# Block-quantised feed-forward: maxima one iteration ahead, scales on GpSimd, gated values three iterations behind

## What is computed

```python
def fp4_quant_dequant(x):                  # blocks of 16 columns
    xb = x.reshape(shape[:-1] + (shape[-1] // 16, 16))
    scale = jnp.maximum(jnp.max(jnp.abs(xb), axis=-1, keepdims=True) / 6.0, 1e-12)
    xn = xb / scale
    idx = jnp.searchsorted(_MID, jnp.abs(xn))
    return (_GRID[idx] * jnp.sign(xn) * scale).reshape(shape)   # grid 0 0.5 1 1.5 2 3 4 6

def fp4_linear(x, w):
    return jnp.einsum('bsk,nk->bsn', fp4_quant_dequant(x), fp4_quant_dequant(w))

h = jax.nn.silu(fp4_linear(x, w_gate)) * fp4_linear(x, w_up)    # 128 -> 352
return fp4_linear(h, w_down)                                    # 352 -> 128
# x = x + 0.5 * ffn(layernorm(x))
```

## Time and profile before

| | us |
|---|---|
| median of 3 runs (1597.82 to 1600.06) | 1597.97 |
| span of the profiled execution | 1594.8 |
| what the median has beside the span | 3.2 |
| first feed-forward, first block maxima to last statistics | 138.24 |
| second feed-forward, the same | 138.29 |
| busy over the span: TensorE, VectorE, ScalarE, GpSimd | 1233.0, 996.9, 714.1, 593.8 |

### The profile page before, as it was taken

How to read it: one execution, slowest core, us unless ns; L and a number is a source line. 1 busy time by engine, 2 the same in 40 slices (tenths; PEclk the granted TensorE clock), 3 DMA queues, 4 the chain that set the end, 5 groups by cost and what they waited for, 6 DMA issues and landing times.

```text
span 1594.8 us, 31915 instructions
## 1 busy us (share of the span) xinstructions
PE 1233.0 (77%) x10217; PEld 799.1 (50%) x10218; DVE 996.9 (63%) x1974; ACT 714.1 (45%) x1328; POOL 593.8 (37%) x859
## 2 busy tenths in 40 slices
PE   0677479999956776299999915999998728999992
PEld 0355346666634556156666602455554525666661
DVE  5799679999838994822222257889896382223233
ACT  0444225555554442144444451666666323444445
POOL 2122221121101220056565614676775104656561
PEclk9989769999988996589999956999999658999996
DMA  8000034223200001011111133434242101111115
GB/s 254 9 0 0 1 61 63 49 53 60 43 2 1 0 0 53 2 36 42 40 39 40 41 112 67 68 56 79 56 75 34 54 0 32 40 40 41 38 41 171
DMA packets 161956, 75.54 MB, mean 47 GB/s; under 512 B 126539, under 2 KB 153940, under 8 KB 161876
## 3 DMA queue, kind: packets, MB, share of 16 engines
q1 hardware_dynamic: 152404, 55.06, 16.1%
q0 software_dynamic: 9472, 19.42, 4.1%
HBM read 28.69 MB, written 15.86 MB: 28 GB/s over the span
## 4 chain that ended last, share of the span: by engine, by line
PE 54%; DVE 25%; issue 7%; ACT 6%; POOL 3%; DMA 3%; SPq 1%; DVEq 1%; POOLq 0%; ACTq 0%
PE PS L990 16%; PE PS L1016 9%; PE PS L656 4%; PE PS L1006 4%; PE PS L358 2%; DVE sg L790 2%; DVE m L790 2%; PE PS L622 2%; PE PS L638 2%; PE PS L575 2%; PE PS L951 2%; DVE q_amax L266 2%; PE PS L610 1%; ACT pt L1070 1%; SPq L882 1%
## 5 line engine op out<-in xcount | busy, mean ns | idle before, releaser
L990 PE MATMUL PS<-wgu,xTs 128*128 x584 | 303.2, 603 | 4.2 <-issue 3.1
L1114 DVE TENSOR_TENSOR pt<-pt,PS 128x512 f32<-128x512 f32 x146 | 100.5, 688 | 295.4 <-PE PS L990 295.4
L715 ACT ACTIVATE pt<-PS 128x768 f32<-128x768 f32 (+1 forms) x256 | 227.5, 917 | 107.8 <-PE PS L638 56.1
L1227 POOL DMA_INDIRECT xs<-rows,src x152 | 147.8, 972 | 192.9 <-DVE src L1108 147.1
L1236 POOL DMA_INDIRECT outs<-ys,dst x144 | 142.4, 989 | 158.5 <-DVE ys L1122 153.0
L1052 ACT ACTIVATE pt<-PS 128x512 f32<-128x512 f32 x146 | 87.2, 597 | 233.8 <-PE PS L990 233.8
L1016 PEld LDWEIGHTS PS<-wdn,pt 128*128 128x128 f32 x1152 | 139.5, 191 | 55.4 <-issue 55.4
L1016 PE MATMUL PS<-wdn,pt 128*128 x1152 | 162.9, 284 | 0.4 <-issue 0.4
L790 DVE TENSOR_REDUCE m<-PS 128x4 f32<-128x1024 f32 x128 | 149.1, 1218 | 10.5 <-PE PS L575 9.9
L575 PE MATMUL PS<-tables 64*128 64x128 bf16 (+2 forms) x1536 | 131.7, 251 | 0.0
L790 DVE TENSOR_REDUCE sg<-PS 128x6 f32<-128x768 f32 x128 | 117.6, 953 | 20.9 <-PE PS L575 20.0
(11 more groups left out here) (229 smaller groups left out, 2239.5 us busy)
## 6 DMA issues: line engine op xcount, KB each, us to landing
pt<-outs SPq DMA_DIRECT2D x16, 512.0 KB, 5.0
rows<-qT SPq DMA_DIRECT2D x12, 256.0 KB, 2.4
xs<-rows,src POOLq DMA_INDIRECT x152, 2.5
outs<-ys,dst POOLq DMA_INDIRECT x144, 2.3
wgu<-in_L_ffn_w_gate SPq DMA_DIRECT2D x1, 2048.0 KB
wgu<-in_L_ffn_w_up SPq DMA_DIRECT2D x1, 2048.0 KB
wdn<-in_L_ffn_w_down SPq DMA_DIRECT2D x8, 256.0 KB
qT<-hqT SPq DMA_DIRECT2D x128, 4.0 KB
```

Of the source, the lines that this page charges most:

```text
L715: s.activation(k.pt[:, a % 4, :, 0:w], k.PS[:, self.bank:self.bank + 2, 0:w], ACT.Exp, scale=self.scale).then_inc(self.s_p, 1)
L990: t.matmul(k.PS[:, 1 + 2 * p + w, :], k.xTs[:, p, :], k.wgu[:, w, ds(e, 1), :].squeeze(1), start=True, stop=True).then_inc((self.s_gate_ps ...
L1114: v.tensor_tensor(k.hs[:, p, :], k.sgs[:, p, :], k.PS[:, 2 + 2 * p, :], ALU.mult).then_inc(self.s_h, 1)
L1227: g.indirect_dma_start(k.xs[:, i % RING, :], None, k.rows[:, :], bass.IndirectOffsetOnAxis(ap=k.src[:, i:i + 1], axis=0)).then_inc(self.s_ ...
```

## The change

Four things are rearranged inside `Ffn`; the arithmetic stays, apart from the order in which the inverse and its factors are multiplied.

1. The block maxima of iteration z + 1 are taken during iteration z, between the gate and the roundings, and their reciprocal directly after them (of the maximum, no more of the scale).
2. The scales, and the inverses' constant factor, are computed by GpSimd (`scales`), ahead of its dequantisations of iteration z. VectorE's multiplication waits for them (`s_inv`).
3. The gated values are rounded three iterations behind x instead of two. On VectorE the order is now multiplication, gate, maxima of the next iteration, roundings, addition.
4. On TensorE the order is now transposes of x, transposes of the gated values, the first half of gate and up, down, the second half. ScalarE's order follows: copy of x, squares, copies of the gated values, normalisation of z + 3, silu.

The diff, without the constructor's new semaphores and the changed loop bounds (N + 4 steps instead of N + 5, four passes of the loop instead of five):

```diff
     def vector(self, eng, ch):
...
-            ch.run(v.tensor_reduce(amax, blocks, AX.X, ALU.max, apply_absolute_value=True))
...
-            ch.run(v.tensor_scalar(scale, amax, -1.0 / 6.0, -1e-12, ALU.mult, ALU.min))
-            ch.run(v.reciprocal(inv, scale))
-            ch.run(v.tensor_scalar(inv, inv, -NUDGE, None, ALU.mult))
-            last = v.tensor_tensor(xn.rearrange("p (n k) -> p n k", k=BLK), blocks,
-                                   inv.unsqueeze(2).broadcast_to([P, n, BLK]), ALU.mult)
-            last.then_inc(self.s_xn_read, 1)
+        def largest(z, p):
+            c = self.cols(z)
+            if self.has(z):
+                eng.wait_ge(self.s_xn, x0 + z + 1)
+            if self.has(z - 3):
+                eng.wait_ge(self.s_h, x0 + z - 2)
             b = slice(c.start // BLK, c.stop // BLK)
...
+            ch.run(v.tensor_reduce(k.qt["amax"][:, b], blocks(k.fxh[p][:, c]), AX.X, ALU.max, apply_absolute_value=True))
+            v.reciprocal(k.qt["inv"][:, b], k.qt["amax"][:, b]).then_inc(self.s_amax, 1)
+        largest(0, 0)
 
         def fn(z, p):
-            if self.has(z) or self.has(z - 2):
-                quantised(z, p)
+            if self.group(z):
...
+                eng.wait_ge(self.s_inv, q0 + z + 1)
+                v.tensor_tensor(blocks(xn), blocks(k.fxh[p][:, c]),
+                                k.qt["inv"][:, b].unsqueeze(2).broadcast_to([P, b.stop - b.start, BLK]),
+                                ALU.mult).then_inc(self.s_xn_read, 1)
+            if self.has(z - 2):
+                eng.wait_ge(self.s_silu, x0 + z - 1)
+                v.tensor_tensor(k.fxh[1 - p][:, HID:k.FW].rearrange("p (a b) -> p a b", a=2), k.sg[:, :, :],
+                                k.PS[:, 2:4, 0:I0], ALU.mult).then_inc(self.s_h, 1)
+            if self.group(z + 1):
+                largest(z + 1, 1 - p)
+            if self.group(z):
+                eng.wait_ge(self.s_sq, q0 + z + 1)
+                ch.run(v.scalar_tensor_tensor(xn, mg, BASE, xn, ALU.add, ALU.add))
+                v.scalar_tensor_tensor(mg, mg, BASE, xn, ALU.add, ALU.subtract).then_inc(self.s_rounded, 1)
             if self.has(z - 4):
                 self.add(eng, z - 4)
...
@@ gpsimd
+        def scales(z, p):
+            c = self.cols(z)
+            b = slice(c.start // BLK, c.stop // BLK)
+            scale = k.fscale[:, p, b]
+            eng.wait_ge(self.s_amax, q0 + z + 1)
+            if self.has(z - 2):
+                eng.wait_ge(self.s_xq, x0 + z - 1)
+            if self.has(z - 5):
+                eng.wait_ge(self.s_hq, x0 + z - 4)
+            eng.sem_inc(self.s_seen, 1)
+            inv = k.qt["inv"][:, b]
+            g.tensor_scalar(scale, k.qt["amax"][:, b], -1.0 / 6.0, -1e-12, ALU.mult, ALU.min)
+            g.tensor_scalar(inv, inv, 6.0 * NUDGE, 1e12 * NUDGE, ALU.mult, ALU.min).then_inc(self.s_inv, 1)
+        scales(0, 0)
...
-            x, h = self.has(z), self.has(z - 2)
+            x, h = self.has(z), self.has(z - 3)
+            if self.group(z + 1):
+                scales(z + 1, 1 - p)
             if x or h:
                 eng.wait_ge(self.s_rounded, q0 + z + 1)
...
@@ tensor, its new order
+            if x:
+                eng.wait_ge(self.s_xqT, x0 + z + 1)
+                if self.later(z):
+                    eng.wait_ge(self.s_h, x0 + z)
+                gate_up(0)
+            if h:
                 eng.wait_ge(self.s_hqT, x0 + z - 2)
                 if self.later(z - 3):
                     eng.wait_ge(self.s_added, x0 + z - 3)
...
                 last.then_inc(self.s_y_ps, 1)
             if x:
...
+                gate_up(1).then_inc(self.s_gu_ps, 1)
```

More of the change, by code:

```diff
@@ L202 @@
     N = NT // 2
[L203 removed]
+    STEPS, FIRST = N + 4, 4
     HID = 2 * D
@@ L233, in later, with group, cols @@
         return self.run or not isinstance(i, int) or i >= n
+    def group(self, z):
+        return self.has(z) or self.has(z - 3)
+    def cols(self, z):
+        return slice(0 if self.has(z) else self.HID, self.k.FW if self.has(z - 3) else self.HID)
     def walk(self, eng, fn, ch=None, per=0):
@@ L332, in tensor, with gate_up @@
         x0, HID = self.x0, self.HID
-        def fn(z, p):
-            x, h, down = self.has(z), self.has(z - 2), self.has(z - 3)
-            if down:
+        def gate_up(j):
+            for w, bank in ((0, 0), (1, 2)):
+                last = t.matmul(k.PS[:, bank + j, 0:I0], k.xqT[:, j * P:(j + 1) * P], k.wguT[:, w, :],
+                                start=True, stop=True)
+            return last
+        def fn(z, p):
+            x, h = self.has(z), self.has(z - 3)
+            if x:
+                eng.wait_ge(self.s_xq, x0 + z + 1)
+                if self.later(z):
+                    eng.wait_ge(self.s_xqT, x0 + z)
+                for j in range(2):
+                    last = t.transpose(k.PS[:, 4, j * P:(j + 1) * P], k.xhq[:, j * D:(j + 1) * D], k.ident[:, :])
+                last.then_inc(self.s_xqT_ps, 1)
+            if h:
+                eng.wait_ge(self.s_hq, x0 + z - 2)
+                if self.later(z - 3):
+                    eng.wait_ge(self.s_hqT, x0 + z - 3)
+                for j in range(2):
+                    for c, (o, w) in enumerate(HC):
+                        o += HID + j * I0
+                        last = t.transpose(k.PS[0:w, 5 + j, c * P:(c + 1) * P], k.xhq[:, o:o + w], k.ident[:, :])
+                last.then_inc(self.s_hqT_ps, 1)
+            if x:
+                eng.wait_ge(self.s_xqT, x0 + z + 1)
+                if self.later(z):
+                    eng.wait_ge(self.s_h, x0 + z)
+                gate_up(0)
+            if h:
                 eng.wait_ge(self.s_hqT, x0 + z - 2)
@@ L381, in normalised, with squared @@
             ins.then_inc(self.s_xn, 1)
+        def squared(z, p):
+            if self.group(z):
+                c = self.cols(z)
+                eng.wait_ge(self.s_xn_read, q0 + z + 1)
+                if self.has(z) and self.later(z, 2):
+                    eng.wait_ge(self.s_xq, x0 + z - 1)
+                if self.has(z - 5):
+                    eng.wait_ge(self.s_hq, x0 + z - 4)
+                s.activation(k.fmg[p][:, c], k.fxn[p][:, c], ACT.Square, scale=BINADE ** 0.5).then_inc(self.s_sq, 1)
         eng.wait_ge(self.k.sem("statistics_ready"), self.phase + 1)
@@ L385, in scalar @@
         normalised(1, 1)
-        def squared(z, p):
-            if self.has(z) or self.has(z - 2):
-                c = slice(0 if self.has(z) else HID, k.FW if self.has(z - 2) else HID)
-                eng.wait_ge(self.s_xn_read, q0 + z + 1)
-                if self.has(z) and self.later(z, 2):
-                    eng.wait_ge(self.s_xq, x0 + z - 1)
-                if self.has(z - 4) or (self.has(z - 2) and self.run):
-                    eng.wait_ge(self.s_hq, x0 + z - 3)
-                s.activation(k.fmg[p][:, c], k.fxn[p][:, c], ACT.Square, scale=BINADE ** 0.5).then_inc(self.s_sq, 1)
         squared(0, 0)
+        normalised(2, 0)
         def fn(z, p):
```

84 lines of the change are left out of this document (21 added, 63 removed).

## The result

| | us |
|---|---|
| kernel before, median of 13 runs (1597.55 to 1602.03) | 1598.97 |
| changed kernel, median of 13 runs (1600.02 to 1608.62) | 1604.61 |
| ratio, 95% interval | 1.0032 (1.0021 to 1.0042) |
| changed kernel, profiled span | 1602.1 |

The time lies in the predicted range, 1587 to 1606, but the forecast, 1596 and no change that can be told, is wrong: the kernel is slower by 3.4 to 6.7 us.

The account below looks back on a forecast made before the run. VectorE, 92% busy, bounds the stages: full steps 7.92 us against 7.82, but shorter steps at the ends save 0.9 us a stage. Span 1594.8 - 1.8 = 1593.0, plus 3.2, gives 1596 us; range 1587 to 1606.

Parts of the forecast that it names:

- the bound, and what is removed: Feed-forward stages: VectorE bounds the iteration; scales, factor, gap and wait for squares go, 0.90 us less, 6.92 undisturbed.
- the port: Way to SBUF that VectorE instructions with two SBUF operands and GpSimd instructions take in turns; the second asking waits.
- the collision: VectorE's multiplication waits for GpSimd's 704-column dequantisation and ends at 3.11 instead of 2.11 us, so steps take 7.92.
- the 704 columns: GpSimd's second dequantisation, of the gated values that down multiplies; forecast to go ahead of the multiplication.
- ends at R + 0.72, so the 704-column one is asked for about 0.25 us ahead: GpSimd's 256-column dequantisation, taken as 0.57 us, ends early enough for the 704-column one to precede VectorE's multiplication.
- R: End of VectorE's second rounding, from which the times of a step are counted.
- The small instruction: GpSimd's added instruction on 60 columns, for scales or factor: 0.3 us each, the second ending about R + 0.15.
- Rival one: Multiplication gets in front of the 704-column dequantisation or does not contend: steps of 6.92 to 7.1 us; chance 0.16.
- a late addition only uses up the time for which the multiplication would have waited anyway. I put this at nothing here: TensorE's slow-clock spells, adding up to about 2.4 us, cost nothing because the multiplication would wait at the port anyway.
- hidden room of down: TensorE's down ends at 6.87 us after the rounding, 0.97 us before the addition wants it at 7.84.
- start and end: Stage's filling and draining: first gate about 0.3 us later, shorter steps at both ends, last rounding to end unchanged, 6.40.
- rival two: Small GpSimd instructions land on VectorE's path: 0.1 to 0.5 us a full step, 1599 to 1608 us; chance 0.17.

Follow-up runs that it names:

- factor on ScalarE: Changed kernel with the inverses' factor moved from GpSimd to ScalarE, without the guard for a block of zeros: 1597.63 us, 0.9993 of the kernel before.
- busy TensorE: Changed kernel with TensorE also transposing the identity into unread PSUM columns in three of its waits: 1592.83 us, 0.9957 of the kernel before.
- addition behind the gate: Changed kernel with the addition and its statistics moved from behind the roundings to behind the next step's gate: 1620.47 us, 1.0141 of the kernel before.
- addition ahead of the roundings: Changed kernel with the addition, of the product five iterations back, between reciprocal and roundings on VectorE: 1595.80 us, 0.9983 of the kernel before.
- both orders changed: Kernel with VectorE's addition ahead of the roundings, with TensorE's and ScalarE's orders changed besides: 1580.89 us, 0.9881 of the kernel before.

## Why the prediction was wrong, point by point

**Right: the bound, and what is removed.** VectorE's own work and its waits at the port set the steps in which no addition waits for down. Where the multiplication isn't held off such a step is 6.89 us; the prediction took 6.92.

**Right: the collision.** Where the multiplication stands behind the 704 columns it takes 1.9 to 2.2 us and ends 1 us after them. With the factor on ScalarE all steps are of that kind, 7.87 us against the forecast 7.92, and the time is 1597.6 against 1596: the port's arithmetic was sound where its conditions held.

**The step that failed first: "ends at R + 0.72, so the 704-column one is asked for about 0.25 us ahead".** Three terms were a little short. The small instruction, priced 0.3, is 0.41 by itself (the undisturbed ones at 102.27 and 102.75 above), and 0.41 less the 0.14 of hidden start-up is the 0.28 that it ends behind R. A hand-over of 0.07 follows, counted as nothing. The 256 columns are 0.62, not 0.57. Together 0.13 + 0.07 + 0.05 = 0.25 us: the whole margin. Rival one was told with a single cause, a small instruction of 0.55 us; three small shortfalls do the same. Which of the two steps comes is then decided by the 0.2 us by which the loop's turn delays the multiplication.

**The step that failed second, and made it slower: "a late addition only uses up the time for which the multiplication would have waited anyway. I put this at nothing here".** Both the hidden room of down (0.97 us) and this cover belong to the step where the multiplication waits. Where it doesn't, the addition wants down 1.26 us sooner (R + 6.81, not R + 8.07), while the 704 columns end 1.0 us later and keep down about where it was: at the full clock it ends at R + 7.03 where the multiplication waits (step from R = 107.14), and at R + 6.88 where it doesn't (step from R = 100.25, the addition waits 0.15 us). In a slow spell the lower clock has its full price, 1.3 to 2.9 us. So in a slow spell the short step of 6.89 us is followed by a long one: 8.95 and 8.77 us in the first stage, 9.05, 10.18 and 9.88 in the second, where the clock is lowest; at the full clock by one of 8.15. A short and a long step together are 15.0 us where the addition waits 0.15 us, 15.8 where it waits 1.8, which is twice the forecast's 7.92, and 16.8 to 17.1 where it waits 2.9: of these pairs only the last lose against the forecast. The factor on ScalarE shows the other side: there the cover held, and waits of 0.59 to 0.74 us cost nothing. Rival one had the gain and a ring through silu, but not that the displaced 704 columns take down with them.

**Mis-sized: start and end.** Ten full steps of a stage are 78.3 and 83.2 us, forecast 79.2. The first of them alone is 10.03 and 10.34, because its addition waits 3.04 and 3.34 us. From the last rounding to a stage's end are 8.2 and 8.0 us, forecast as unchanged, 6.40. The last two downs both run at the lower level there (granted clock 0.50 from 168 to 178), where before the last one took 1.60 us. The changed kernel:

```profile
168.33 2.93 PE L393 MATMUL PS<-wdT,hqT 128*128 128x128 f32 x12 [0.95 <-ACT hqT L439]
...
171.30 0.42 DVE L306 SCALAR_TENSOR_TENSOR X<-PS,X 128x256 f32<-128x256 f32 x1 [2.10 <-PE PS L393]
...
173.50 2.93 PE L393 MATMUL PS<-wdT,hqT 128*128 128x128 f32 x12 [0.95 <-ACT hqT L439]
176.46 0.42 DVE L306 SCALAR_TENSOR_TENSOR X<-PS,X 128x256 f32<-128x256 f32 x1 [4.21 <-PE PS L393]
```

The kernel before:

```profile
175.26 1.60 PE L342 MATMUL PS<-wdT,hqT 128*128 128x128 f32 x12 [0.95 <-ACT hqT L418]
```

The short steps were some 0.8 us a stage cheaper than forecast, the first gate ended 0.3 and 0.6 us later. Worked out: 2 x 137.4 = 274.8 forecast; + 3.2 (full steps) - 1.7 (short ones) + 3.4 (ends) + 0.9 (first gates) = 280.6, which is what the two windows show.

**Right against rival two.** Roundings stayed at 1.09 and 1.16 us in the full steps: the small instructions cost VectorE nothing directly. They cost it by their place ahead of the dequantisations.

**What stays open.** The displaced columns open the way (0.15 us of wait by themselves), the lower clock makes the wait (1.3 to 2.9 us); what decides when the clock falls was not separated. The granted clock is 0.89 and 0.82 here and 0.93 and 0.88 with the factor on ScalarE, whose TensorE waits some 0.9 us for the 704 columns instead of 1.9; but one wait of 1.91 us was followed by the full clock. The busy TensorE raises the clock but also fills TensorE's queue, and its profiled execution (1598.5 us) is longer than its median run. Why the addition behind the gate lands on steps of 10 us, where the addition ahead of the roundings has mostly 6.7 to 7.4, was only argued: in the one the pair ends at R + 3.3, in the other at R + 2.9. The trace adds that in the long step from R = 77.95 half and down took 2.2 us longer than in the step shown of the other (2.56 and 2.57 us, not 1.35 and 1.54), so that a good part of the difference is the lower clock.

## What to carry to other kernels

When two engines take turns at a port, work out who asks first with every small instruction and hand-over in the sum, and treat a margin as small as the sum of their errors (here 0.25 us) as an open order: cost both. Then ask of the loser in each order who waits for it: a displaced producer moves the wait to another engine, and a cover that comes from a wait is gone when the wait is. The order that holds is one in which the bound engine asks first by a clear margin and nothing on its ring hangs on the instruction that it displaces.

## What the runs showed of the hardware

- The port is given in order of asking between two GpSimd instructions that follow each other too: asked for at R + 0.93, while the 256 columns run to R + 0.97, the multiplication gets in ahead of the 704 columns, and takes 1.14 us, about its undisturbed length. The Trainium skill's rule ("SBUF — State Buffer", Who interferes with whom) that issue order decides who waits agrees; by the rows it decides instruction by instruction.
- The GpSimd instruction on 128 x 60 scales takes 0.41 us undisturbed, and 1.00 and 1.14 us in the listing where it waits for a rounding, so listed GpSimd times contain waits at the port.
- More work on TensorE can shorten the time: 224 extra transposes in each stage went with a granted clock of 0.95 and 0.92, instead of 0.89 and 0.82, and the kernel went from 1604.6 to 1592.8 us. With both orders changed, where full steps hardly wait for TensorE, 186 extra ones in each stage took it from 0.93 and 0.90 to 1.00 and 0.94, and the time stayed (1580.9 and 1580.3 us).
